# A four-layer kernel of attention, mixtures and experts on one core: the dense expert's pieces and the score banks of the last two batches

## The reference

```python
x = x + L0_xattn(layernorm(x), ctx, ctx, Wq, bq, Wk, bk, Wv, bv, Wo, bo)   # 16 heads of 16, softmax(q k^T / 4) v
x = x + L0_ffn(layernorm(x), P_w, U1, U2, U3, W1, W2, b2)
#   C1, C2, C3: softmax over the 3 largest of 12 expert scores, per row
#   h = gelu(sum_e C1[:, e] * (x @ W1[e].T));  y = sum_e C2[:, e] * (h @ W2[e].T) + C3 @ b2
x = x + L1_xattn(layernorm(x), ctx, ctx)                                    # 16 heads, no projections
x = x + L1_ffn(layernorm(x), router_w, w_gate, w_up, w_down, ws_gate_up, ws_down)
#   probs = softmax(x @ router_w.T); the 8 largest of 64 experts, weights renormalised
#   each expert takes at most 128 rows, in row order; pos = running count of earlier rows of that expert
#   routed = sum over the row's experts of weight * (silu(x Wg) * (x Wu)) @ Wd
#   shared = silu(x Wsg) * (x Wsu) @ Wsd                                     # the dense expert, for every row
#   routed + shared
```

## Time and profile before

| what | before |
|---|---|
| median of 3 runs | 3038.3 us |
| profiled execution, its own time | 3023.01 us |
| its span, first to last instruction | 3021.2 us |
| mean granted clock of TensorE | 0.955 |
| PE busy | 2738.9 us (91%) |
| DVE busy | 2202.1 us (73%) |
| ACT busy | 1039.7 us (34%) |
| POOL busy | 820.5 us (27%) |

### The profile page before, as it was taken

How to read it: one execution, slowest core, us unless ns; L and a number is a source line. 1 busy time by engine, 2 the same in 40 slices (tenths; PEclk the granted TensorE clock), 3 DMA queues, 4 the chain that set the end, 5 groups by cost and what they waited for, 6 DMA issues and landing times. The chain is left out here.

```text
span 3021.2 us, 61482 instructions
## 1 busy us (share of the span) xinstructions
PE 2738.9 (91%) x23816; PEld 2297.6 (76%) x23816; DVE 2202.1 (73%) x5944; ACT 1039.7 (34%) x1524; POOL 820.5 (27%) x858
## 2 busy tenths in 40 slices
PE   2599999999999999999999999999999999956886
PEld 1388888888888888888888888888888888736775
DVE  2467888887888887888888888888888888733332
ACT  1223433333334333333333333333333333211111
POOL 1000122222222222222222222222222222334334
PEclk7599999999999999999999999999999999967998
DMA  6633444443333333333333333333333331117785
GB/s 196 183 87 97 114 124 111 116 116 110 108 96 89 100 100 100 94 86 94 100 95 94 100 89 100 98 89 83 97 99 100 99 90 43 40 39 211 207 213 126
DMA packets 321183, 327.31 MB, mean 108 GB/s; under 512 B 45405, under 2 KB 302231, under 8 KB 320892
## 3 DMA queue, kind: packets, MB, share of 16 engines
q1 hardware_dynamic: 287100, 304.20, 35.6%
q0 software_dynamic: 33792, 19.17, 3.6%
HBM read 182.18 MB, written 212.37 MB: 131 GB/s over the span
## 5 line engine op out<-in xcount | busy, mean ns | idle before, releaser
L653 ACT ACTIVATE exps<-second 128x1024 f32<-128x1024 f32 x512 | 525.9, 1027 | 785.0 <-PE second L1135 777.1
L548 POOL DMA_INDIRECT expert_slots<-row_mem,sidx x512 | 509.1, 994 | 790.9 <-PE first L1117 553.8
L1215 PE MATMUL mixp<-w_h,r_part_h 128*128 128x256 f32 x3072 | 668.5, 299 | 40.1 <-DVE hid L906 24.0
L822 DVE TENSOR_REDUCE nm<-first 128x4 f32<-128x1024 f32 x512 | 623.2, 1217 | 93.1 <-PE first L1117 93.0
L1215 PE MATMUL mixp<-w_h,r_part_l 128*128 128x256 f32 x3072 | 609.7, 280 | 0.0
L1215 PE MATMUL mixp<-w_l,r_part_h 128*128 128x256 f32 x3072 | 609.3, 279 | 0.0
L1215 PEld LDWEIGHTS mixp<-w_h,r_part_h 128*128 128x128 f32 x3072 | 467.4, 189 | 97.0 <-DVE hid L906 31.7
L1215 PEld LDWEIGHTS mixp<-w_l,r_part_h 128*128 128x128 f32 x3072 | 468.4, 188 | 0.0
L1215 PEld LDWEIGHTS mixp<-w_h,r_part_l 128*128 128x128 f32 x3072 | 468.1, 188 | 0.0
L906 DVE SCALAR_TENSOR_TENSOR x_mem<-mixp,C,x_mem 128x256 f32<-128x256 f32 x768 | 329.6, 477 | 114.6 <-PE mixp L1215 114.2
L906 DVE SCALAR_TENSOR_TENSOR hid<-mixp,C,hid 128x256 f32<-128x256 f32 x704 | 300.7, 474 | 35.8 <-PE mixp L1215 33.8
(11 more groups left out here) (211 smaller groups left out, 3687.0 us busy)
## 6 DMA issues: line engine op xcount, KB each, us to landing
kst<-k_parts SPq DMA_DIRECT2D x256, 192.0 KB, 3.8
qst<-q_parts SPq DMA_DIRECT2D x256, 192.0 KB, 4.1
q_parts<-nat_h SPq DMA_DIRECT2D x128, 256.0 KB
k_parts<-ctx_part_h SPq DMA_DIRECT2D x64, 256.0 KB, 2.4
k_parts<-nat_h SPq DMA_DIRECT2D x64, 256.0 KB, 2.4
q_parts<-nat_l SPq DMA_DIRECT2D x64, 256.0 KB
exps<-in_wgu SPq DMA_DIRECT2D x39, 384.0 KB, 4.4
expert_slots<-row_mem SPq DMA_DIRECT2D x8, 1284.0 KB, 12.5
```

Source lines behind the costliest of these rows:

```text
L548: pool.e.indirect_dma_start(out=slots_dram, out_offset=bass.IndirectOffsetOnAxis(ap=sidx[b % 2][:, t, k:k + 1], axis=0), in_=row[b % 2][:, ...
L653: act.e.activation(exps[:, j % NU, :, :, :].rearrange("p k t s -> p (k t s)"), second[:, :, :].rearrange("p k s -> p (k s)"), ACT.Exp, sca ...
L822: dve.e.tensor_reduce(nm[u % 2][:, :, 2 * j:2 * j + 2].rearrange("p t k -> p k t"), first[:, :, :].rearrange("p k (t s) -> p k t s", t=TIL ...
L1215: m = pe.e.matmul(mixp[q % 2][:, t * D:(t + 1) * D], src[i][:, dt, t * P:(t + 1) * P], wmix[n][j][:, l, dt, :], start=(k == 0), stop=(k == ...
```

## The change

Batches 30 and 31 get places of their own for `d_gate`, `d_up` and `d_down`, and in the second attention of batch 31 the second and fourth `s1` pair of each half writes the two `mixp` banks in place of `first`. The two `mixp` banks become one tensor, as `first` and `second` are. The experts' first use of `mixp` waits for all score maxima.

```diff
+LAST = {2: {"d_gate": 174.6, "d_up": 181, "d_down": 196.6}, 1: {"d_gate": 157, "d_up": 157.1, "d_down": 163.62}}
...
-        for what, p in PLACES.items():
+        for what, p in {**PLACES, **LAST.get(NB - b, {})}.items():
...
-        mixp = [ps(f"mixp{i}") for i in range(2)]
-        first, second = (ctx.enter_context(nc.psum_tensor(n, [P, 2, 512], F32)) for n in ("first", "second"))
-        bank1, bank2 = ([mem[:, k, :] for k in range(2)] for mem in (first, second))
+        mixp_mem, first, second = (ctx.enter_context(nc.psum_tensor(n, [P, 2, 512], F32)) for n in ("mixp", "first", "second"))
+        mixp, bank1, bank2 = ([mem[:, k, :] for k in range(2)] for mem in (mixp_mem, first, second))
...
+        def in_mixp(b, kind, j):
+
+            return kind == "C" and b == NB - 1 and j % 2 == 1
...  vector_program, "s1"
-                                        first[:, :, :].rearrange("p k (t s) -> p k t s", t=TILES), AX_X, ALU.max,
+                                        (mixp_mem if in_mixp(b, kind, j) else first)[:, :, :].rearrange(
+                                            "p k (t s) -> p k t s", t=TILES), AX_X, ALU.max,
...  tensor_program, "s1"
-                    claim("first", (v_max, 4 * u + j + 1))
+                    if in_mixp(b, kind, j):
+                        pe.wait_ge(v_mix, 4 * L * NB)
+                        pe.wait_ge(v_max, 4 * u + j - 1)
+                        bank = mixp
+                    else:
+                        claim("first", (v_max, 4 * u + j + 1))
+                        bank = bank1
...
-                            m = pe.e.matmul(bank1[k][:, t * S:(t + 1) * S], q_st[u % 3][at, j, t * P:(t + 1) * P],
+                            m = pe.e.matmul(bank[k][:, t * S:(t + 1) * S], q_st[u % 3][at, j, t * P:(t + 1) * P],
...  tensor_program, "e_gate"
+                    pe.wait_ge(v_max, 4 * HALVES)
```

## The result

The changed kernel takes 3025.1 us, the median of 8 runs (3021.27 to 3036.76), against 3036.9 us for the kernel before beside it (8 runs, 3033.5 to 3046.7): ratio 0.9962 [0.9946, 0.9977], 11.7 us less. The forecast was 12.0 us less.

What follows compares the result with a forecast made beforehand. It took the end to be bound by the experts' chain of DMA round trips, whose start follows batch 31's mask. Last attention 6.7 plus routing 5.3 made 12.0 us, 3038.3 to 3026.3 us; range 3021 to 3034.

Steps and rivals of the forecast that it cites:

- A: Last attention, first pair of unit 126 to `misc` free: 47.43 us before, forecast 40.7.
- B: Routing, from `misc` free to the end of batch 31's mask: 17.16 us before, forecast 11.85.
- C: Scatters and row request, from batch 31's mask to the first expert's turn: 28.41 us before, forecast 28.4.
- D: Experts' stage, first expert's turn to the end of the span: 275.3 us before, forecast 275.3.
- (a): Maxima of unit 126: PE fills one bank set while DVE reads the other, gain 1.2 us, bounds 0 and 2.7.
- (b): Fourth reduction of unit 126 to the first `s2`: `s2` at 2665.7, 5.2 us earlier, (a) included.
- rival of a late landing: Maxima's DMAs land late in unit 126, `s2` still at 2670.9: 5.2 us lost, 3031.5 us, chance 0.08.
- (c): Four `s2` and `av` after unit 126's maxima: 10.3 us in place of 12.06, gain 1.8 us.
- stretch one: The last attention, 2652.9 to 2700.3 us: 6.7 us earlier, bounds 4.2 and 7.9.
- rival that they earn nothing: Second banks in the last attention give no gain: 9.7 us off in all, 3028.6 us, chance 0.10.
- Stretch two: Batch 31's routing, `misc` free to the mask: 11.85 us, gain 5.3, bounds 3.0 and 6.0.
- rival that its chain takes the whole gain back: Experts' stage: longer waits in the chain of combining DMAs eat the gain, 3037 us, chance 0.14.

Runs made afterwards that it cites:

- e1: The changed kernel again, no edit: 3022.99 us, ratio 0.9958 to the kernel before.
- e4: The changed kernel with only batch 31's dense expert moved, batch 30's at its old place and no second banks: 3031.33 us, ratio 0.9988 to the kernel before.
- e9: The changed kernel once more, no edit, on the chip of the third group: 3026.71 us, ratio 0.9946 to the kernel before.
- e3: The changed kernel with the second banks only, the dense expert at its old places: 3034.26 us, ratio 0.9986 to the kernel before.
- e2: The changed kernel with the dense expert's new places only, all pairs in `first`: 3023.02 us, ratio 0.9956 to the kernel before.
- e7: The changed kernel plus 43 matmuls that nobody reads, to hold the clock: 3025.37 us, ratio 0.9954 to the kernel before.
- e5: The changed kernel with batch 30's dense expert also behind batch 31's routing, using a separate buffer for turned rows: 3036.43 us, ratio 0.9990 to the kernel before.
- e11: e8 without batch 30's 16 scatters, whose rows never reach the experts: 3020.12 us, ratio 0.9940 to the kernel before.
- e8: The changed kernel with the edits of e5 and e6, and three experts' weight loads ahead of the stores: 3027.25 us, ratio 0.9956 to the kernel before.
- e10: The changed kernel with each scatter of batch 30 waiting for the `s2` piece ahead of it: 3023.35 us, ratio 0.9950 to the kernel before.
- e12: The changed kernel with the edits of e8 and e10 together: 3023.00 us, ratio 0.9953 to the kernel before.
- e6: The changed kernel with batch 30's 16 scatters placed closer together, before the last attention ends: 3028.54 us, ratio 0.9969 to the kernel before.

## Why the prediction was right, point by point

**The sum.** 11.7 us measured for 12.0, with an interval of 7.0 to 16.4 (1 - 0.9977 and 1 - 0.9946 of 3036.9): that it is so close is in part luck. In the profiles the two lengths that the forecast priced gave 10.2 us together (A 1.6 short of it, B 0.2), and C and D, for which it had nothing, gave 1.0. From the first pair to the end the three profiles of the changed kernel take 357.1, 357.0 and 360.6 us, 11.2, 11.3 and 7.7 less than the one before.

**What bounds the end.** Right. C and the count of scatters behind the mask did not move in e1 to e4 (28.38 to 28.44), while B moved from 10.6 to 17.7 and the turn went with it. Between executions C is less rigid than I had it: 29.12 in e9.

**(a) Pairs of unit 126.** Forecast 1.2 us less to the end of the fourth reduction; 7.62 us against 8.92 is 1.3 less.

**(b) First `s2`.** Forecast 12.8 us behind the first pair, 12.56 measured: issue 1.36 after the reduction, landing 3.58 us where I took 3.71 from the other unit. The rival of a late landing falls: in eleven of the thirteen profiles since it was 3.58 or 3.59, and e3 and e4, where it reads 5.89 and 6.71, have PE in the dense expert at that time. Of 5.46 us won here, 4.15 come from the places alone (e2).

**(c) `s2` and `av`.** Forecast 10.3 us, 10.08 measured.

**The rest of stretch one.** Here a term was missing. I said that it keeps its length but for 0.3 us. First `s2` of unit 127 to `misc` free did so (12.85 for 12.56), but `av` to that `s2` went from 4.79 to 6.81 us, the late starts of ScalarE. Without them (e1) A is 40.12, 0.6 us better than forecast; with them 42.30, 1.6 worse.

**The second banks.** Forecast 2.2 us, measured 1.8 (e2 against e1, neither with late starts). The rival that they earn nothing is refuted for A, though the whole times, 0.9956 and 0.9958, can't tell the two kernels apart. The sentence of the Trainium skill (TensorE: Matmul & The Clock Gate, HAM oscillation) that double-buffering of PSUM gave no further gain does not carry over to this stretch, where VectorE's reduction of 1.23 us had stood in line with PE's 0.80.

**The clock.** Pricing `s2` and `av` at 1.2 GHz was right, and e3 shows the price: with the products in front, an `s2` takes 0.41 us. Busy time by stretch after (us, PE, PEld, DVE, ACT, POOL, granted clock, DMA, GB/s), over `d_gate`, `d_up` and the turn with the logits:

```profile
2706.40:2709.90 3.50, 3.44 (x8) 2.38 (x9) 1.25 (x7) 0.00 (x0) 1.98 (x2) 0.50 0.00 0
2709.90:2713.40 3.50, 3.50 (x13) 2.38 (x11) 1.45 (x4) 0.59 (x1) 2.84 (x3) 0.62 0.02 0
2713.40:2716.40 3.00, 1.30 (x10) 0.97 (x8) 1.13 (x3) 0.89 (x2) 2.21 (x3) 1.00 0.03 3
```

It rises inside `d_up`, as in the earlier trace rows, and turn and logits run at the high level, as priced. The rule of the Trainium skill (same page, Part 1), that sustained activity releases the throttle, agrees with this. What it gives back can be lost at once: in e7 it was high under 20 extra matmuls and low again behind 4.64 us of idle PE, when the real work came.

**Stretch two.** Forecast 11.85 us, within 10.57 to 12.06 for the same program. Its terms were 6.4 to the turn, 3.45 to the end of the exponential and 2.0 to the mask; after has 6.60, 3.37 and 2.09. What spreads it is where in `d_gate` and `d_up` the clock rises: `d_up` took 3.18 us in one profile and 1.89 in another, and I had allowed 2.17 to 2.79.

**What comes behind.** Forecast: last sum some 16.5 us behind the mask, measured 15.90; the loads were issued by 2737.67 (2737.24 + 0.43), 6.8 us before the rows were asked for. I had counted 9 us of room to the last sum and it was 10.1, but the loads use 3 of it. e5 shows what is behind that edge, once late starts of 8.2 us had pushed it there.

**The experts' stage.** D 274.5 for 275.3. The rival that its chain takes the whole gain back falls with the whole times, all three of which keep the gain. That it takes a part is not excluded: D is 277.8 and 278.1 in the same program (e1, e9), and for before there is one value.

## What to carry to other kernels

Count from the last stage backwards: a rigid row of issues turns every microsecond of its first release into one at the end, and dense work that nobody waits for can stand behind that release, up to the point where a store or load of the next stage queues behind it. Take a stretch apart by lengths counted from one instruction of the trace, since here two spans of equal length hid a difference of 11 us. Gains of two edits that remove the same wait don't add (4.3 and 5.5 made 7.3).

## What the runs showed of the hardware

With GpSimd issuing indirect DMAs without a break (0.97 us each and 0.30 between), steps of ScalarE started up to 2.7 us after what released them, and steps of VectorE 4.1 and 4.2 us (e5); the trace names nothing that they waited for (`<-remote`, or a product long done). Taking the scatters away removed it all in the last attention (e11 against e8). Where the row was broken, ScalarE was nearly on time (0.63 and 0.02 in e10) or on time (the exponentials of e12).

It is not the row alone. e1 and e2 had such a row at the same steps and were on time, and e1 had its last ten scatters within 0.02 us of where the late execution of the same kernel had them, counted from the end of `av`. Before, e3 and e4 were on time beside such a row as well, but they differ in one more thing, which the DMA view shows: in after and in the ten other runs a load of instructions (8 KB, queue q14) starts within 0.3 us of the end of the exponential ahead of the copy, and in before, e3 and e4 none falls there. For the first two steps the count is then: row and load, late in seven profiles of nine; row without load, in none of three; load without a row across the steps (e10, e11), 0.63 us in one and nothing in the other. That a load held up by the scatters' traffic delays ScalarE would fit this, but no run tests it, and no such load stands near the late exponentials of e8 or within 3 us of the late steps of VectorE in e5. What decides it stays open. The late starts do explain where e6 and e8 lost their gain, and that a piece moved off the path beside such a row isn't free.
